# Second-layer V, GNN and output products as split single passes, layer norm without its scale, joined small loads

## Reference

```python
xn = layernorm(x)
x  = x + gnn0(xn) + attention0(xn)
x  = x + experts0(layernorm(x))          # 8 experts, 32 tokens each, 1024 wide
xn = layernorm(x)
x  = x + relu(poly(adj) @ (xn @ W + b)) + (attention1(xn) @ W_out + b_out)
x  = x + swiglu_experts(layernorm(x))    # 1 shared + 16 experts, 1365 wide, top 4
```

## Time and profile before

| | us |
|---|---|
| median of three runs (546.28 to 546.48) | 546.46 |
| the profiled execution | 549.87 |
| its span, first to last instruction | 548.1 |
| PE busy | 525.9 (96%) |
| DVE busy | 423.3 (77%) |
| ACT busy | 331.4 (60%) |
| POOL busy | 6.2 (1%) |

### The profile page before, as it was taken

One profiled execution on the slowest core, in us unless ns is written; L12 is line 12 of the kernel. 1 busy time (PEld: TensorE's weight loads), 2 busy tenths in 40 slices (PEclk: granted clock), 3 DMA queues, 4 the chain that ended last, 5 costly groups with the idle time before them and its releaser, 6 DMA issues.

```text
span 548.1 us, 7339 instructions
## 1 busy us (share of the span) xinstructions
PE 525.9 (96%) x2577; PEld 400.3 (73%) x2577; DVE 423.3 (77%) x414; ACT 331.4 (60%) x300; POOL 6.2 (1%) x32
## 2 busy tenths in 40 slices
PE   7999898699899999999999999999999999999997
PEld 4674332145688888888888888888888888888785
DVE  7724510025999989899998999989898989999983
ACT  1102000025388777787887778777787878778761
POOL 2000000000000000000000000000000000000000
PEclk9988999789999999999999999999999999999999
DMA  8999999999899999999999999999999999975560
GB/s 295 409 418 422 422 421 422 420 413 399 268 328 370 396 396 308 382 344 360 374 339 372 326 386 366 340 362 338 395 350 354 336 342 402 345 320 194 223 212 19
DMA packets 37079, 190.35 MB, mean 347 GB/s; under 512 B 4779, under 2 KB 4779, under 8 KB 31428
## 3 DMA queue, kind: packets, MB, share of 16 engines
q1 hardware_dynamic: 36288, 189.96, 90.6%
q10 hardware_dynamic: 772, 0.13, 0.1%
HBM read 189.81 MB, written 0.26 MB: 347 GB/s over the span
## 4 chain that ended last, share of the span: by engine, by line
PE 86%; DMA 7%; DVE 3%; issue 2%; ACT 1%; POOL 0%; POOLq 0%; DVEq 0%; ACTq 0%
PE ps L1314 30%; PE ps L1352 22%; PE ps L1318 15%; DMA w_set<-in_w 5%; PE ps L1052 4%; PE ps L1336 3%; PE ps L1124 1%; PE ps L1203 1%; PE ps L1045 1%; PE ps L1220 1%; PE ps L1112 1%; DMA w_raw<-in_w 1%; DVE s_lo L767 1%; PE ps L1102 1%; PE ps L1116 1%
## 5 line engine op out<-in xcount | busy, mean ns | idle before, releaser
L755 DVE TENSOR_TENSOR s_lo<-w_raw,s_hi 128x1365 fp32r<-128x1365 f32 x136 | 208.6, 1577 | 12.2 <-ACT s_hi L580 12.0
L580 ACT CAST s_hi<-w_raw 128x1365 fp32r<-128x1365 f32 x136 | 180.7, 1337 | 31.9 <-PE ps L1318 18.3
L1314 PE MATMUL ps<-s_hi,xT_hi 128*128 128x512 f32 (+1 forms) x408 | 153.1, 375 | 1.9 <-DVE hT_lo L950 1.2
L1314 PE MATMUL ps<-s_lo,xT_hi 128*128 128x512 f32 (+1 forms) x408 | 149.1, 368 | 0.0
L767 DVE TENSOR_TENSOR s_lo<-w_raw,s_hi 128x1536 fp32r<-128x1536 f32 x68 | 105.8, 1578 | 2.3 <-ACT s_hi L592 2.3
L1318 PE MATMUL ps<-s_hi,xT_lo 128*128 128x512 f32 (+1 forms) x408 | 106.1, 368 | 0.0
L592 ACT CAST s_hi<-w_raw 128x1536 fp32r<-128x1536 f32 x68 | 91.2, 1345 | 22.2 <-PE ps L1318 18.2
L1314 PEld LDWEIGHTS ps<-s_hi,xT_hi 128*128 128x128 f32 x408 | 76.6, 188 | 18.7 <-DVE hT_lo L950 1.4
L1314 PEld LDWEIGHTS ps<-s_lo,xT_hi 128*128 128x128 f32 x408 | 76.7, 188 | 12.2
L1318 PEld LDWEIGHTS ps<-s_hi,xT_lo 128*128 128x128 f32 x408 | 72.6, 188 | 5.8
L1352 PE MATMUL ps<-s_hi,hT_hi 128*128 128x512 f32 (+1 forms) x182 | 73.5, 404 | 0.6 <-DVE hT_lo L950 0.6
(11 more groups left out here) (191 smaller groups left out, 303.9 us busy)
## 6 DMA issues: line engine op xcount, KB each, us to landing
w_raw<-in_w SPq DMA_DIRECT2D x128, 682.5 KB, 6.2
w_raw<-in_w SPq DMA_DIRECT2D x51, 768.0 KB, 6.1
w_set<-in_w SPq DMA_DIRECT2D x32, 1024.0 KB, 26.5
w_raw<-in_w SPq DMA_DIRECT2D x12, 512.0 KB, 6.2
w_raw<-in_sw SPq DMA_DIRECT2D x8, 682.5 KB, 16.8
wk_sb<-in_wk SPq DMA_DIRECT2D x2, 1024.0 KB, 16.6
wq_sb<-in_wq SPq DMA_DIRECT2D x2, 1024.0 KB, 18.9
gcn_sb<-in_gcn_w SPq DMA_DIRECT2D x2, 1024.0 KB, 14.6
```

The costliest lines, as they stand in the source:

```text
L580: a.copy(s_hi[pair][:, 0:F1], raw[:]).then_inc(hi_ready, 1)
L755: v.tensor_tensor(s_lo[pair][:, 0:F1], raw[:], s_hi[pair][:, 0:F1].bitcast(F32), ALU.subtract).then_inc(lo_ready, 1)
L1314: mm(bank(i + c0 // D)[:, 0:even(n)], xT_hi[:, k], w[:, c0:c0 + even(n)], start=(k == 0 and w is hi), stop=False)
```

## The change

Three things change. (1) Layer norms 2 and 3 only subtract the mean (`centre`); the factor `rstd` is applied later, per row, wherever it is needed. For queries, whose product comes out transposed, a fifth transpose on PE spreads `rstd` over a PSUM tile and DVE scales `xnT` with it into `xsT`. (2) The value, GNN and output products of layer 1 become three single-pass products each (`split_product`): high parts of the weights are cast by ACT, the remainder of V by DVE, those of GNN and output by POOL, in place over the raw weight. Two scratch pairs of the experts move, and waits on POOL and ACT move with them. (3) The dummy products around the waits of layer 0 are dealt out anew, SP loads V before Q, and seven small loads become one.

```diff
-            for t, (to, w, landed) in enumerate(((wk1_sb, wk1, ld_k), (wq1_sb, wq1, ld_q), (wv1_sb, wv1, ld_v),
-                                                 (gnn_w_sb, gnn_w, ld_gnn_w))):
+            for t, to, w, landed in ((0, wk1_sb, wk1, ld_k), (2, wv1_sb, wv1, ld_v), (1, wq1_sb, wq1, ld_q),
+                                     (3, gnn_w_sb, gnn_w, ld_gnn_w)):
...
             pool.wait_ge(ffn0_ps, GROUPS)
-            clear_pads(range(4))
+            clear_pads(range(2))
+
+            def split_rest(name):
+
+                pool.wait_ge(split_hi_ready[name], 1)
+                pg.tensor_tensor(flat(split_lo[name]), flat(split_raw[name]), flat(split_hi[name]).bitcast(F32),
+                                 ALU.subtract).then_inc(split_lo_ready[name], 1)
+
+            split_rest("gnn")
+            split_rest("out")
+            pool.wait_ge(k_ps, 2)
+            pool.wait_ge(v_ps, 2)
             pool.wait_ge(q_ps, 2)
-            clear_pads(range(4, 5))
-            pool.wait_ge(y_ps, 2)
-            clear_pads(range(5, PAIRS_N))
+            clear_pads(range(2, 4))
+            pool.wait_ge(wout_ps, 1)
+            clear_pads(range(4, PAIRS_N))
...
+            def centre(l, x_in):
+                then(v.bn_stats(stats[:], x_in))
+                then(v.bn_aggr(mean_var[:], stats[:]))
+                v.tensor_scalar(xn[:], x_in, mean_var[:, 0:1], None, ALU.subtract).then_inc(xn_ready, 1)
+                v.tensor_scalar(var_eps[:], mean_var[:, 1:2], LN_EPS, None, ALU.add).then_inc(var_ready, 1)
...
+            def scaled_keys():
+
+                dve.wait_ge(k_ps, 2)
+                dve.wait_ge(rstd_ready, 3)
+                v.tensor_scalar(neg_k[:], bank(3), rstd[:], 0.0, ALU.mult, ALU.min).then_inc(negk_ready, 1)
+                then(v.tensor_scalar(k_phi[:], bank(3), rstd[:], 0.0, ALU.mult, ALU.max))
+                dve.wait_ge(expk_ready, 2)
+                v.tensor_tensor(k_phi[:], k_phi[:], neg_k[:], ALU.add).then_inc(kphi_ready, 1)
...
+            def split_product(name, to, rows, rows_lo, done, steps, cols=slice(0, D)):
+
+                for i in steps:
+                    k = i % KT
+                    if i == 0:
+                        pe.wait_ge(split_hi_ready[name], 1)
+                    if i == KT:
+                        pe.wait_ge(*rows_lo)
+                    if i == 2 * KT:
+                        pe.wait_ge(split_lo_ready[name], 1)
+                    w = split_lo[name] if i >= 2 * KT else split_hi[name]
+                    last = mm(to, rows[i // KT % 2][:, k], w[:, k, cols], start=(i == 0), stop=(i == 3 * KT - 1))
+                if 3 * KT - 1 in steps:
+                    last.then_inc(done, 1)
...
             transpose_mid(1, 1)
+            keep_warm(1, 1)
             pe.wait_ge(midT_ready, 4)
-            for t in range(KT):
+            for t in range(KT - 1):
                 ffn_down(1, 1, t)
+                keep_warm(1, 1)
+            ffn_down(1, 1, KT - 1)
             scatter_out(1)
-            keep_warm(3, 1)
+            keep_warm(2, 1)
...
-            keep_warm(3, 1)
+            keep_warm(2, 1)
             transpose_x(3, 4)
...
-                    mm(bank(7)[:, 0:E1], ones[0:1, :], gate1_b[:], start=False, stop=True).then_inc(gate1_ps, 1)
+                    last.then_inc(gate1_ps, 1)
```

More of the change, by code:

```diff
@@ L58 @@
 SLOTS = 5
+SMALL = (3 * ET, 2 * KT, 4, KT * E0, KT * E1, E1)
 SETS = 2 * GROUPS * CHUNKS0
@@ L534, in copy_v @@
                 act.wait_ge(v_ps, l + 1)
-                a.copy(v_aug[:, :, 0:DH], bank(4).rearrange("p (h v) -> p h v", h=HEADS)).then_inc(v_ready, 1)
+                v_in = bank(4).rearrange("p (h v) -> p h v", h=HEADS)
+                if l == 0:
+                    a.copy(v_aug[:, :, 0:DH], v_in).then_inc(v_ready, 1)
+                else:
+                    act.wait_ge(rstd_ready, 3)
+                    a.activation(v_aug[:, :, 0:DH], v_in, ACT.Copy, scale=rstd[:]).then_inc(v_ready, 1)
             def copy_ah(i):
@@ L598, in silu @@
                     act.wait_ge(h_ready, e)
-                a.activation(act_a[:], row_of(0), ACT.Silu).then_inc(act_ready, 1)
+                else:
+                    act.wait_ge(rstd_ready, 4)
+                a.activation(act_a[:], row_of(0), ACT.Silu, scale=rstd[:]).then_inc(act_ready, 1)
             def hT_to_hi(e, c, kind):
@@ L972, in router @@
                 then(v.reciprocal(small[:, 7:8], small[:, 6:7]))
-                then(v.tensor_scalar(w, w, small[:, 7:8], None, ALU.mult))
+                then(v.tensor_scalar(w, w, small[:, 7:8], rstd[:], ALU.mult, ALU.mult))
             lo_w2(0, 0)
@@ L1039, in transpose_x, with project_q @@
                 last.then_inc(xnT_ps, 1)
-            def project_q(w, ms=range(KT)):
+            def project_q(w, rows, ms=range(KT)):
                 for m in ms:
                     for k in range(KT):
-                        last = mm(tiles(2)[:, m], w[:, k, P * m:P * m + P], xnT[:, k], start=(k == 0), stop=(k == KT - 1))
+                        last = mm(tiles(2)[:, m], w[:, k, P * m:P * m + P], rows[:, k], start=(k == 0), stop=(k == KT - 1))
                 if KT - 1 in ms:
@@ L1135, in _ @@
             count_edges(1)
-            project_q(wq0_sb)
+            project_q(wq0_sb, xnT)
             count_edges(2)
@@ L1297, in _ @@
             mm(bank(7), polyT[:], y[:], start=True, stop=True).then_inc(gnn1_ps, 1)
-            pe.wait_ge(ld_wout, 16)
-            pe.wait_ge(mixT_ready, 1)
-            for k in range(KT):
-                last = mm(bank(2), mixT[:, k], wout_sb[:, k], start=(k == 0), stop=(k == KT - 1))
-            last.then_inc(wout_ps, 1)
-            keep_warm(3, 1)
+            pe.wait_ge(mixT_hi_ready, 1)
+            split_product("out", bank(2), (mixT_hi, mixT_lo), (mixT_lo_ready, 1), wout_ps, range(3 * KT))
+            keep_warm(2, 1)
             transpose_x(3, 4)
@@ L1434, in laid_out @@
     w2_0 = i["L0_ffn_W2"].reshape(GROUPS, EG, CHUNKS0, KT, P, D).transpose(0, 2, 4, 3, 1, 5)
+    small = [i[k].reshape(P, ET).view(np.float32) for k in ("src", "dst", "edge_weight")]
+    small += [i["L0_gnn_b_gcn"].reshape(2 * KT, P).T, np.tile(i["L1_gnn_diffusion_weights"], (P, 1))]
+    small += [by_tile(i[k]).reshape(P, -1) for k in ("L0_ffn_Wg", "L1_ffn_gate_w")]
+    small += [np.tile(i["L1_ffn_routing_bias"], (P, 1))]
     return {
-        "x": i["x"], "edges": np.stack([i[k].reshape(P, ET).view(np.float32) for k in ("src", "dst", "edge_weight")], axis=1),
+        "x": i["x"], "small_in": np.concatenate(small, axis=1),
         "gcn_w": np.stack([by_tile(w) for w in gcn_w]),
-        "gcn_bT": i["L0_gnn_b_gcn"].reshape(2, KT, P).transpose(2, 0, 1),
         "mlp_w": np.stack([by_tile(w) for w in mlp_w]),
```

125 lines of the change are left out of this document (77 added, 48 removed).

## The result

Twelve runs of the kernel after have a median of **546.07 us** (544.26 to 547.49). Twelve runs of the kernel before on the same chip have 547.85 (546.28 to 549.88), and three of those are the runs that the prediction was given (546.46). The ratio is 0.996, with a 95% interval of 0.9943 to 0.9977: faster, by 0.4%. The forecast was 541.3, the range 539.8 to 545.0, so the median lies 1.1 us above the range. The profiled execution took 544.88 us, span 543.2. Against the profiled one of before (549.87, span 548.1) that is a gain of 4.9 in the span, where the sum had said 5.1.

What follows compares the result with a forecast made beforehand. Bound: weight-tile DMA to 104.55 us, then a 37.0 us gap the change acts on, then PE's rigid expert passes. Terms -6.0 (gap), -0.3 (loads), +1.2 (clock) sum to -5.1: 546.46 to 541.3 us, range 539.8 to 545.0.

Steps and rivals of the forecast that it cites:

- the median lies 3.4 below the profiled one and gets the same difference: Whole kernel: the profiled execution's -5.1 us is taken off the earlier median, 546.46, giving 541.3.
- the 6.0 us that I took off: Gap from last weight tile to layer 1's experts: their first product at 135.55 instead of 141.58 us.
- the joined loads: Small loads at the start: fewer packets free DMA before the last tile, -0.3 us (0 to 0.5).
- rival B: Layer 1: POOL's GNN remainder holds up DVE's bias-row sum once; +2.9 us, 544.2 in all; chance 0.17.
- each wait for a tile at 2.5 us and 1.96 us of work in it: Layer 0's last tiles: products plus one dummy fit each wait, keeping PE's clock at the upper level.
- the way from keys to experts: Layer 1, from the keys' first product to the experts' first: 25.0 us, where before took 26.9.
- POOL's remainder inside its bounds: Layer 1's GNN and output weight remainders: 5.0 us each, bounds 3.5 to 6.9; up to 5.6 costs nothing.
- the splits of three products: V, GNN and output products: three single-pass products each save at most 1.9 to 2.3 us of PE.
- the clock fall ahead of the experts: Just before layer 1's experts: PE has little work, so its clock falls, costing +1.2 us.
- Rival A: Layer 0's last tiles: clock falls anyway at 102.1, dummies hurt; gain only 2.3 us, 544.2; chance 0.18.
- C: Layer 1: POOL keeps DVE out for both remainders, +7.9 us, 549.2, slower; chance 0.05.
- D: Experts: their weights come late, so nothing in the gap matters; same time, 546.2; chance 0.02.

Runs made afterwards that it cites:

- e1: The kernel before, unchanged, run again: 546.72 us, ratio 0.9986.
- e9: The kernel before with only the new places of layer 0's dummy products: 546.49 us, ratio 0.9968.
- e15: The kernel before with the small loads joined, except the transposed GCN bias, loaded apart: 547.06 us (one run).
- e16: The kernel before with the small loads joined, except the two gates' weights, loaded apart: 544.29 us (one run).
- e4: The kernel before with the small loads joined into one and nothing else: 544.94 us, ratio 0.9969.
- e11: The kernel after, unchanged, run again: 545.62 us, ratio 0.9957.
- e10: The kernel after with two dummies instead of four between layer 0's last tiles and four instead of two ahead of the experts: 544.31 us, ratio 0.9931.
- e13: The kernel after with DVE's sum of x2 and the output bias moved behind the step `y`: 543.44 us, ratio 0.9921.
- e17: The kernel before with the small loads joined, except the broadcast of the four diffusion weights, loaded apart: 548.10 us (one run).
- e7: The kernel after with DVE's sum of x2 and the output bias moved one step back, behind the diagonal's copies: 545.67 us (one run).
- e6: The kernel after with V, GNN and output products as single float32 products again: 544.30 us, ratio 0.9924.
- e12: The kernel after with float32 V, GNN and output products, two dummies between the tiles and four ahead of the experts: 543.90 us, ratio 0.9932.
- e8: The kernel before with four more broadcast loads, issued by ACT behind its first five loads: 550.06 us (one run).
- e2: The kernel after with four instead of two dummies ahead of the second layer's experts: 545.83 us, ratio 0.9964.
- e14: The kernel after with DVE's bias sum behind `y`, two dummies between the tiles and four ahead of the experts: 542.65 us, ratio 0.9906.

## Why the prediction was wrong

**The base, the step "the median lies 3.4 below the profiled one and gets the same difference", failed.** The 3.4 were the distance of two groups of executions (e1), and both profiles of the upper one have the clock fall at 102. Of the 6.0 us that I took off, some 3 were that fall, and e9 shows them to be worth 3 in the upper group and nothing in the lower. A difference read from the upper group was subtracted from the median of the lower. Before's own median over twelve runs is 547.85. That no profile of before's lower group was taken is a gap: that the place of the fall is what parts the groups rests on e9, in which the upper one vanished, and on the pair e15 and e16. Nor is this step the whole miss: without the 3 the sum is -2.1 and the forecast 544.4, still 1.7 below the median, though the joined loads gave 1.6 more than I had. e4 and e9 each reach with one step (0.9969 and 0.9968) nearly what the whole change does (0.996), so other steps of it cost time. The profiles show two such costs, rival B and the dummies. How the median's shortfall divides between them is open.

**Rival B came true in part of the executions, and I gave it 0.17.** In the profile of after the sum went first, by 1.15 us; in e11, the same program, it came second by 0.4, at a price of 3.3 us of the way (28.5 for 25.2), where I had 2.9. The 0.4 on top may be the clock, which fell in PE's new wait. The mechanism was told rightly, the near tie (118.4 and 118.35 in the prediction) too; the weighing was not. Each gain ahead of the tie brings POOL's start forward and not the bias row, which hangs on the tile: the better the rest goes, the surer the collision. It came second in one of the two profiles of the kernel after, and in e10. That taking the sum out of POOL's way brings the median ratio from 0.996 to 0.9921 (e13) suggests that it is common. How common I can't say, as only profiled executions show it. The Trainium skill, page "SBUF — State Buffer", section "Who interferes with whom", has the rule that DVE's and GpSimd's shared port pair is an exclusive lock. These runs agree, with 4.70 and 2.29 us for a sum of 0.68, and 0.87 for a copy from PSUM in the midst of it. (The 4.5 us that the prediction calls that page's stand on the page named last in this part.)

**The joined loads were mis-sized: 0.3 in the prediction, 1.9 measured (e4).** I priced them by the queue's share of the engines' time, 0.1% of the span. What they cost was the stream beside them: 295 GB/s in the first fortieth of the span for 340 after. Two thirds is the broadcast (e17).

**A cost was missed: dummies in the way of late products.** I had each wait for a tile at 2.5 us and 1.96 us of work in it, so that nothing came later. That holds while PE is ahead of the stream. In the profile of after it was not: its first keys products, in the head, took 3.78 us for 1.98 in before, half speed, though the records have a clock of 1.00 in that stretch. The head alone does not decide it: e7, with 3.62 there, was nearly in time, and its clock stayed at 1.00 in 38 to 42 us, where after has 0.62 and e6 0.50. PE came late to the last tiles and ran products and dummies back to back, 2.05 us a tile where the stream takes 2.5, so that it made up only 0.45 us with each: the last tile was there at about 102.7 (as in the profiles where PE waits for it), its products began at 104.76. In e6, with the same dummies, they began at 105.43. In e11, e13 and e7, with the same dummies and PE in time or nearly so, they began at 102.75 to 102.86. So in after's profile +2.1 of lateness with dummies hid -1.9 of joined loads, and keys came 0.24 from where I had them by luck, for two wrong reasons.

**Right were:** the clock held up through the waits (1.00 in 98.7 to 105.5, e9 for that alone); the way from keys to experts, 25.0 predicted and 25.15 measured; within it DVE as the one that `x3` waits for; the centred layer norm (1.66 from `x3` to `xn` for 1.65; `var_eps` and the power are off the chain, transposes start 0.54 behind `xn`); POOL's remainder inside its bounds, 4.55 for 5.0; the splits of three products, 1.1 in the prediction (5.2 at `x3` less 4.1 at the keys) and 0.9 to 1.5 by e6 and e12; the clock fall ahead of the experts, in kind, but about 0.7 of the predicted 1.2. Rival A shows in no profile with after's dummies. Neither does C: in e11 DVE's sum got in between POOL's two remainders, and the second took 4.99 for 4.57. D did not show, as the experts' start moved with what stands before it. The 4497 ns that the Trainium skill gives on the page "GPSIMD Engine Reference", section "Elementwise — side-by-side cycle accounting", are within 0.06 us of the 4.55 measured for the remainder.

By that ledger the profiled pair is -3.9 at the keys, -1.75 on the way, +0.75 behind it (406.5 us from the experts' first product to the end before, 407.3 after): -4.9. Two slips of the prediction change nothing: 578 of the 772 packets went, three quarters and not two thirds, and by its own sum C decides for slower from 4.2 us for a remainder on, not 4.3.

## What to carry to other kernels

Before a difference is subtracted from a median, ask which group of the kernel's executions the profile shows: two repeats of the unchanged kernel, with the clock of the stretch in question and not its mean, might have told here that 3 of my 5 us were there to be had in half of the executions only. When two engines that exclude each other start within a microsecond, take it that they collide, and move the short step to where the long one is over, if it has no hurry. A filler for the clock belongs only where the engine surely waits; where it may be late, it is on the path.

## What the hardware showed that I had not expected

- One load of 16 bytes broadcast to 128 partitions, beside the weight stream at the start, cost 1.2 us of the stream (e17: 230 GB/s in 6 to 8 us for 392), while four more of them, issued later, cost 0.3 (e8).
- POOL's power of a single column (`rstd`) took 1.85 us beside DVE's difference of 1.52, for 0.55 when alone (after, 134.65 and 109.54). It has a single column, and waited for the whole of DVE's operation all the same.
- PE products in the head ran at half speed in some executions (3.78 us in after, 3.62 in e7, for 1.98), where the granted clock of the profile's rows is 1.00. In e2 and e14 the same products take 3.30 and 3.17, and there the rows of 8 to 12 us have 0.53 to 0.62.
- A fall of the clock while PE waits for tiles costs under 0.2 us at the keys (e16, 109.80 for 109.63 in e4); one just behind the last tile costs 2.6 more (e15, 112.36).
